# Masks made on GpSimd, exponentials over 2048 columns and a value bias that joins the residual, in a graph attention layer

## What is computed

```python
h = jnp.maximum(_layernorm(x, axis=-1), 0.0)
neib_att = jnp.tanh(neigh @ Wn1 + bn1) @ Wn2 + bn2      # 4096 x 32
value = neigh @ Wv + bv                                  # 4096 x 128
x_att = jnp.tanh(h @ Wx1 + bx1) @ Wx2 + bx2              # 4096 x 32
ws = leaky_relu(x_att @ neib_att.T, 0.01)                # 4096 x 4096
ws = softmax(where(adj > 0, ws, -9e15), axis=1)
out = x + concatenate([h @ Wfx + bfx, ws @ value], axis=1)
```

## Time and profile before

| | |
|---|---|
| median of 3 runs | 562.13 us (561.35 to 564.34) |
| span of the profiled execution | 562.6 us |
| steps 19 to 123, from their first to their last adjacency load | 385.0 us, 7.40 us for two steps |

### The profile page before, as it was taken

One profiled execution on the slowest core, in us unless ns is written; L12 is line 12 of the kernel. 1 busy time (PEld: TensorE's weight loads), 2 busy tenths in 40 slices (PEclk: granted clock), 3 DMA queues, 4 the chain that ended last, 5 costly groups with the idle time before them and its releaser, 6 DMA issues.

```text
span 562.6 us, 9958 instructions
## 1 busy us (share of the span) xinstructions
PE 523.6 (93%) x2780; PEld 386.5 (69%) x2823; DVE 493.3 (88%) x883; ACT 459.2 (82%) x713; POOL 197.5 (35%) x310
## 2 busy tenths in 40 slices
PE   5897999889999999999997999999999999989996
PEld 4455756666787677776775667776877777667874
DVE  2769757799999999999997899999999999997654
ACT  2653667899899898999897889999899999999653
POOL 1410012134444445444533444355434444431000
PEclk9989999999999999999999999999999999999999
DMA  7842753445446633564465344664455445530100
GB/s 202 222 141 54 136 114 51 96 78 113 76 76 123 139 61 59 113 149 73 76 115 130 60 76 76 130 131 75 64 109 109 68 72 96 113 66 2 38 1 20
DMA packets 38019, 52.02 MB, mean 92 GB/s; under 512 B 3920, under 2 KB 29776, under 8 KB 37968
## 3 DMA queue, kind: packets, MB, share of 16 engines
q0 software_dynamic: 9216, 33.56, 36.4%
q1 hardware_dynamic: 28752, 17.90, 10.7%
HBM read 80.81 MB, written 4.19 MB: 151 GB/s over the span
## 4 chain that ended last, share of the span: by engine, by line
PE 32%; issue 31%; POOL 14%; DVE 10%; ACT 4%; DMA 2%; POOLq 1%; DVEq 1%; SPq 0%
POOL scores L417 8%; PE ps_turned L878 6%; PE ps_scores L856 4%; DVE pt_lo L647 4%; PE ps_turned L785 3%; PE ps_product L897 3%; PE ps_product L899 3%; POOL adj_in L399 3%; PE ps_product L898 3%; PE ps_turned L789 2%; ACT scores L505 2%; DVE scores L668 2%; PE ps_scores L855 2%; DMA adj_in<-in_adj 1%; DVE mask L634 1%
## 5 line engine op out<-in xcount | busy, mean ns | idle before, releaser
L417 POOL TENSOR_TENSOR scores<-scores,mask 128x512 f32<-128x512 f32 x109 | 126.7, 1162 | 220.6 <-ACT scores L505 220.6
L647 DVE TENSOR_TENSOR pt_lo<-ps_turned,pt_hi 128x512 fp32r<-128x512 f32 x256 | 174.7, 683 | 20.3 <-PE ps_product L899 15.6
L482 ACT ACTIVATE pt_hi<-ps_turned 128x512 fp32r<-128x512 f32 x256 | 153.0, 598 | 34.2 <-PE ps_turned L878 21.4
L878 PE MATMUL ps_turned<-ident,scores 128*128 128x128 f32 x1024 | 158.5, 277 | 13.5 <-DVE pt_lo L647 13.0
L878 PEld LDWEIGHTS ps_turned<-ident,scores 128*128 128x128 f32 x1024 | 119.4, 141 | 63.4 <-DVE pt_lo L647 27.4
L505 ACT ACTIVATE scores<-ps_scores 128x1024 f32<-128x1024 f32 x128 | 131.3, 1026 | 36.3 <-PE ps_scores L856 32.3
L517 ACT ACTIVATE scores<-scores,neg_top 128x1024 f32<-128x1024 f32 x128 | 146.2, 1142 | 0.0
L668 DVE CUSTOM_DVE_ANT_0 scores<-ps_scores,scores,top 128x1024 f32<-128x1024 f32 x96 | 122.2, 1273 | 9.6 <-issue 4.5
L897 PE MATMUL ps_product<-pt_hi,v_hi 128*128 128x512 f32 x256 | 113.6, 444 | 0.2 <-DVE pt_lo L647 0.2
L634 DVE TENSOR_SCALAR mask<-adj_in 128x1024 bf16<-128x1024 bf16 x128 | 106.8, 835 | 7.6 <-PE ps_scores L856 3.8
L856 PE MATMUL ps_scores<-neib,xs 128*128 128x512 f32 x256 | 108.2, 500 | 5.6 <-DVE mask L634 4.5
(11 more groups left out here) (78 smaller groups left out, 407.9 us busy)
## 6 DMA issues: line engine op xcount, KB each, us to landing
adj_in<-in_adj POOLq DMA_DIRECT2D x64, 512.0 KB, 5.5
scores<-in_L_gnn_neigh SPq DMA_DIRECT2D x8, 512.0 KB, 4.2
x_rows<-in_x SPq DMA_DIRECT2D x8, 512.0 KB, 6.2
x_left<-in_x SPq DMA_DIRECT2D x8, 256.0 KB, 6.0
x_right<-in_x SPq DMA_DIRECT2D x8, 256.0 KB, 2.9
out_h<-x_left SPq DMA_DIRECT2D x8, 256.0 KB, 2.3
out_h<-x_right SPq DMA_DIRECT2D x8, 256.0 KB, 5.0
scores<-in_x SPq DMA_DIRECT2D x1, 512.0 KB, 4.7
```

What stands on the lines that cost most here:

```text
L417: pool.tensor_tensor(half, half, mask[:, s % 2, BANK:CHUNK], ALU.add).then_inc(masked, 1)
L482: act.activation(pt_hi[:, (2 * b + u) % HI_RING], pt[:, u], ACT.Copy).then_inc(hi_done, 1)
L647: dve.tensor_tensor(pt_lo[:, u], pt[:, u], pt_hi[:, (2 * b + u) % HI_RING].bitcast(FP32), ALU.subtract).then_inc(lo_done, 1)
L878: last = pe.transpose(pt[:, u, i * P:(i + 1) * P], scores[:, parity * TILES + i, n * P:(n + 1) * P], ident[:, :])
```

## The change

- `mask_of` moves from DVE to Pool. Pool calls it for chunk 0 before its steps, and for chunk s+1 at the very start of step s: ahead of the mask addition of chunk s and of the adjacency load. Its waits stay as they were; the addition gets one more, on the mask of its own chunk.
- The exponential is taken every second step over 2048 columns; its sums and the counts of its semaphore follow.
- The bias products L789 are gone. `b_v` has a tensor of its own, and Pool adds it to `x_right` (`right_sum`, two halves a group, at steps 10 and 11 of a group's sixteen). Since each row of the softmax sums to one, adding the bias to the result is the same as adding it to the values.

```diff
+        def right_due(s):
+            b = s - FIN_LAG - X_RIGHT
+            return b // GSTEPS + 1 if b >= 0 and b % GSTEPS == 0 and b // GSTEPS < GROUPS - 1 else None
...
         @block.gpsimd
-            pool.memset(ones[:, :], 1.0).then_inc(made, 1)
...
+            def right_sum(g, h):
+                pool.wait_ge(x_right_in, 16 * (g + 1))
+                half = x_right[:, h * TILES // 2:(h + 1) * TILES // 2, :]
+                pool.tensor_tensor(half, half, b_v[:, :, :].to_broadcast([P, TILES // 2, D_OUT]), ALU.add).then_inc(
+                    right_summed, 1)
...
+            def mask_of(n, it):
+                k = n + PERIOD * it
+                pool.wait_ge(adj_ready[n % ADJ_RING // LOAD], 16 * (n // ADJ_RING + 1) + 16 * PERIOD // ADJ_RING * it)
+                if n >= 2:
+                    pool.wait_ge(scored, k - 1)
+                if n - 2 >= POOL_MASKS:
+                    pool.wait_ge(masked, k - 1 - POOL_MASKS)
+                pool.sem_inc(pool_joined, 1)
+                pool.tensor_scalar(mask[:, n % 2, :], adj_in[:, n % ADJ_RING, :], 0.0, MASKED, ALU.is_le,
+                                   ALU.mult).then_inc(mask_done, 1)
...
+            pool.wait_ge(wide_in[0], WIDE_IN)
+            for h in range(2):
+                right_sum(0, h)
+            mask_of(0, 0)
 
             def step(s, it):
+                if s < STEPS - 1:
+                    mask_of(s + 1, it)
                 if POOL_MASKS <= s < STEPS:
                     parity, tile, c = chunk_of(s)
                     pool.wait_ge(risen, s + 1 + PERIOD * it)
+                    pool.wait_ge(mask_done, s + 1 + PERIOD * it)
                     half = scores[:, parity * TILES + tile, c * CHUNK + BANK:(c + 1) * CHUNK]
                     pool.tensor_tensor(half, half, mask[:, s % 2, BANK:CHUNK], ALU.add).then_inc(masked, 1)
...
+                for i in range(2):
+                    if (g := right_due(s - i)) is not None:
+                        right_sum(g + 2 * it, i)
...
         @block.scalar
-                if 0 <= e < STEPS:
+                if 0 <= e < STEPS and e % 2 == 0:
...
-                    cols = scores[:, parity * TILES + tile, c * CHUNK:(c + 1) * CHUNK]
+                    cols = scores[:, parity * TILES + tile, c * CHUNK:c * CHUNK + HALF]
                     act.activation(cols, cols, ACT.Exp, bias=neg_top[:, tile % 2, :],
-                                   accum_out=sums[:, parity, tile, c:c + 1]).then_inc(exp_done, 1)
+                                   accum_out=sums[:, parity, tile, c // 2:c // 2 + 1]).then_inc(exp_done, 1)
...
         @block.vector
-                if s < POOL_MASKS:
-                    mask_of(s + 1, it)
...
-                if POOL_MASKS <= s < STEPS - 1:
-                    mask_of(s + 1, it)
...
-                        dve.wait_ge(x_right_in, 16 * (g + 1))
+                        dve.wait_ge(right_summed, 2 * (g + 1))
...
         @block.tensor
-                                         w_v[:, k, :], start=k == 0, stop=False)
-                    last = pe.matmul(ps_value[:, v % 2, i * D_OUT:(i + 1) * D_OUT], ones[:, :], b_v[0:1, 0, :],
-                                     start=False, stop=True)
+                                         w_v[:, k, :], start=k == 0, stop=k == KT - 1)
```

More of the change, by code:

```diff
@@ L60 @@
 EXP_LAG = CHUNKS + 1
+HALF = 2 * CHUNK
+HALVES = N_NEIGH // HALF
 BACK_LAG = GSTEPS + 3
@@ L78 @@
 X_LEFT_LOAD, X_SUM = 4, 9
+X_RIGHT = 6
 V_START, V_STRIDE = 1, 2
@@ L112, in build @@
         ident = sb("ident", [P, P], FP32)
+        b_v = sb("b_v", [P, 1, D_OUT], FP32)
         ident_bf16 = sb("ident_bf16", [P, P], BF16)
@@ L115, in build @@
         neg_top = sb("neg_top", [P, 2, 1], FP32)
-        sums = sb("sums", [P, 2, TILES, CHUNKS], FP32)
+        sums = sb("sums", [P, 2, TILES, HALVES], FP32)
         row_sum = sb("row_sum", [P, TILES], FP32)
@@ L123, in build @@
         b2 = sb("b2", [P, 2], FP32)
-        ones = sb("ones", [1, P], FP32)
         stats = sb("stats", [P, TILES, 6], FP32)
@@ L146, in build @@
         w_v = scratch(5, 0, KT, D_OUT)
-        b_v = scratch(5, 512, 1, D_OUT)
         hidden_stack = pt_hi[:, 0:2, :]
@@ L201, in build @@
         row_sum_done, sums_done = sem("row_sum_done"), sem("sums_done")
-        right_done = sem("right_done")
+        right_summed, right_done = sem("right_summed"), sem("right_done")
         x_right_in = sem("x_right_in")
@@ L572, in neigh_step @@
                     x_stack_low(0, 0, x_bank(0))
-                    mask_of(0, 0)
                 first = it_is(it, e, 0)
@@ L624, in _ @@
             dve.wait_ge(b2_in, B2_IN)
[L626 to L635, removed]
             def lo(s, u, it):
@@ L681, in step @@
                     if n >= 2 * CHUNKS:
-                        dve.wait_ge(exp_done, (n // CHUNKS - 1) * CHUNKS + PERIOD * it)
+                        dve.wait_ge(exp_done, (n // CHUNKS - 1) * HALVES + 2 * TILES * HALVES * it)
                     dve.tensor_scalar(neg_top[:, n // CHUNKS % 2, :], top[:, n // CHUNKS % 2, CHUNKS - 1:CHUNKS],
@@ L704, in step @@
                     parity = b // GSTEPS % 2
-                    dve.wait_ge(exp_done, (g + 1) * GSTEPS)
+                    dve.wait_ge(exp_done, (g + 1) * TILES * HALVES)
                     if b:
@@ L828, in x_wide_layer @@
                     last.then_inc(x_wide, 1)
-            pe.wait_ge(made, 3)
+            pe.wait_ge(made, 2)
             for _ in range(WARM_UP):
@@ L868, in turn @@
                 j = 2 * b + u + 2 * PERIOD * it
-                per_chunk = BLOCKS // CHUNKS
-                if n % per_chunk == 0:
-                    pe.wait_ge(exp_done, (b // GSTEPS + 1) * GSTEPS - CHUNKS + n // per_chunk + 1 + PERIOD * it)
+                per_half = BLOCKS // HALVES
+                if n % per_half == 0:
+                    pe.wait_ge(exp_done, ((b // GSTEPS + 1) * TILES - 1) * HALVES + n // per_half + 1
+                               + 2 * TILES * HALVES * it)
                 if b == 0 and u == 0:
```

## The result

The changed kernel takes 790.3 us (median of 4 runs, 788.6 to 794.1) against 562.3 (4 runs). The ratio is 1.403, with a 95% interval of 1.397 to 1.409. The direction was forecast, the size was not: 598 us, in a range that ended at 652. The profiled execution has a span of 788.1 us.

The account below looks back on a forecast made before the run. The prediction took DVE as the middle stage's limit before, PE in the values stage, and Pool's chain of load, landing, mask, addition after the change. Its terms summed to 524 + 62 M, 598 us at M = 1.2; range 572 to 652.

Parts of the forecast that it names:

- Ring: On Pool, each adjacency load waits for a mask awaiting the previous load's landing: 6.7 + M us a pair, against 7.40.
- the sign that was named: In the profile after, Pool's masks wait for the DMA every second step, some 1 to 2 us each.
- The formula 524 + 62 M: Whole kernel's time in us from the load turns and remaining terms: 598 at M = 1.2, 582 at 0.94, 654 at 2.1.
- M: Time of one Pool mask over 1024 columns: taken as 1.2 us, between 0.94 and 2.1; break-even at 0.7.
- Rival B: Pool's mask goes at a two-input operation's pace or below: 654 us and more; chance 0.22 for 630 to 670.
- DVE relieved of masks: Middle stage: about 0.8 of DVE's 3.6 busy us a step goes; nothing gained while engines wait for Pool.
- Bias products: Stage of the values, where PE is the limit: dropping them frees 13 us of PE, nearly all lost again.
- Exponential: On ACT, 2048 columns take 2.0 us in place of 2 x 1.142: 0.14 us a step less, one accumulator read fewer.
- Rival A: Adjacency loads land sooner without DVE's masks, so loads are not the limit; chance 0.03 about no change, 0.07 clearly faster.
- Rival C: PE's idle waits lower its clock every turn: over 10 us a pair, over 700 us; chance 0.04, shared with dearer masks.
- the estimate by that page: Pool mask at 1.03 cycles an element, 1.2 GHz: 0.88 us and a fixed part, 1.07; sum 591 instead of 598.

Follow-up runs that it names:

- the short masks: Changed kernel with Pool masks made over only the first 256 or 512 of each 1024 columns, the rest left zero: 592.7 and 649.0 us.
- the load put ahead: Adjacency load issued at the start of Pool's step: with 256-column masks 542.9 us against 592.7, with full masks 779.5 against 790.3.
- the kernel with the bias alone: Kernel before, with the value bias added to x's right half on Pool and no bias products on PE: 551.3 us, ratio 0.982.

## Why the prediction was right, and where wrong

- **Ring, and that it makes the change slower: right**, shown by the short masks and by the load put ahead. It would have been enough with a mask of the size that I had in mind; with the mask as it is, Pool's summed work is as long as the ring, and opening the ring gives back 10.8 us only. So the sign that was named, Pool's masks waiting 1 to 2 us every second step, came in part: 27 waits, 17.4 us. The formula 524 + 62 M with the M of those kernels gives 591 and 644; measured 592.7 and 649.0.
- **The failed step is M, the price of a Pool mask: 1.2 us in the sum, 3.64 measured.** By the formula that is 62 x 2.44 = 151 of the 190 us that were missing. I took the affine select (0.73 us for 1000 columns) as the lower and the addition (1.9) as the upper row, as if the price went by the number of tensors read. Measured: 3.36. Only the fixed 0.2 us, from the tensor-scalar of 4 columns, held. A row of 4 columns of the very operation says nothing of its price for a column, and rows of other operations did not bound it. Rival B, the mask "at the pace of a two-input operation, or below", was the true one, but its chance went to 630 to 670 us; all above 670 had 4%, together with the clock. That the direction came out right owes nothing to M: any M above 0.7 gave it.
- **The formula at M = 3.64 gives 750, 38 us short** of the span of 788.1. It counts only the ring, and has no term for Pool's summed work. The load of step 19 came at 137.89 against 134.4 (3.5 us). The middle took 578.4 us against 52 x 10.34 + 14 = 552 (27 us): Pool's own work, 2 x (3.64 + 1.12) + 0.6 = 10.1 us a pair, leaves no gap into which the Newton work and the four sums a group could go, and I had counted the sums as hidden behind the landing; most pairs without them took 10.4 to 10.6 us, those with sums up to 12.2, and the first pair of each Newton work some 13.2. The end took 71.8 us against 63.8 (8 us), since the last four steps go at Pool's pace too.
- **DVE relieved of masks: right that it brings nothing here; its worth without the ring was put too high.** I had 3.4 to 3.5 us a step with the next limit at PE. With the ring open and no masks on DVE at all it was 3.6, and 543 us instead of 533. That kernel has the long exponential, and in it DVE waits 37.3 us for ACT's high parts, 58 times, against 3.4 us in the kernel before. So a part of the 10 us can be the exponential's and not PE's; a kernel that tells them apart was not run. PE is busy 58.1 of 60 us there:

```profile
200.00:260.00 60.00, 58.06 (x324) 44.97 (x325) 47.93 (x90) 52.80 (x72) 47.48 (x65) 1.00 0.56 104
```

- **Bias products: right**, 13 us of PE costed, 12.3 us seen where the ring does not take them back (the load of step 19 in the kernel with the bias alone). In the changed kernel all of it was lost, as the prediction said, and more: its load of step 19 comes at 137.89, before at 111.83.
- **Exponential: size right** (2.0 us), and that it is worth nothing at DVE's limit; the prediction did not foresee that it holds up the high parts.
- **Rival A, faster by earlier landings: fell.** The median landing is 5.4 us in the changed kernel, 5.5 before, with the masks gone from DVE. The one row that was held against the rival says little: 0.60 us for the issue of a load, read there as the mark of a mask running beside it, is the median of all issues in the changed kernel, which has no masks on DVE. The rule of the Trainium skill that was weighed there (SBUF — State Buffer, section "Who interferes with whom") says that a VectorE instruction in a two-port mode and one of GpSimd can't have the shared port pair at once: the one that came first keeps it to its end. The masks agree with it in the kernel before, where those that began beside a Pool instruction ended 0.29 us (median) after it; that the masks run in such a mode no trace shows.
- **Rival C, the clock: it fell, but was not the limit.** Two stretches of the changed kernel:

```profile
283.40:286.80 3.40, 0.01 (x1) 0.02 (x2) 0.67 (x1) 0.60 (x1) 3.40 (x2) 1.00 0.50 100
287.30:290.70 3.40, 3.40 (x12) 2.71 (x11) 1.89 (x3) 1.72 (x3) 2.91 (x6) 0.50 0.01 2
```

PE stood still, waiting for a mask, and then ran at the lower of its levels (0.50 is 1.2 of 2.4 GHz). From 400 to 700 us the clock is 0.94. Pool is busy 96% of that time, so at most the rest, 13 of 300 us, can be the clock's. In the stage of the values the clock is 0.82 with Pool 88% busy. What it costs was not measured apart. The time is over 700 us, as this rival had it, but not by its cause.

The Trainium skill (GPSIMD Engine Reference, section 4.1) calls one-input work on GpSimd roughly line-rate. The copy comes near to that (1.04 us for 1024 columns), the tensor-scalar does not (2.78 and 3.64): the estimate by that page, 1.07 us, was as far off as the 1.2. Its advice to keep elementwise work on VectorE held: the same mask takes 0.42 us on DVE when Pool is not beside it.

## What to carry to other kernels

Before an instruction moves to Pool, measure that very operation at its full width, in a probe behind the kernel's end: neighbouring operations differ by a factor of 3.5 for the same columns. When a consumer moves to the engine that issues its loads, look for the ring load, landing, consumer, next load; it is opened by issuing the load ahead of the consumer, and it can set the pace with an engine that looks half idle. Work out beside it all that the engine itself does in one turn, small work included: the longer of the two sets the turn. A longer instruction that saves fixed time also holds up what is queued behind it, so judge it by who waits there and not by its sum.

## What was not expected of the hardware

- Pool's tensor-scalar takes 0.2 us and 3.36 us for 1000 columns with two operations (3.64 us for 1024), and 2.78 us for 1024 with one, the same in bfloat16 and float32 and for compare, subtract or product; a sum of two tensors 2.11 us for 1024 columns, a copy 1.04.
- A mask on DVE takes 0.41 to 0.43 us; one that begins while a Pool instruction runs ends 0.27 to 0.31 us after that instruction, 0.95 us in the mean (kernel before), while Pool's addition takes 1.16 us as ever. Making it one place later in DVE's order, with the loads moved ahead, was worth 7.6 us of 551.
